# The tanh gate multiplied into the values and their bias once, and the sum of gated attention and x made by GpSimd instead of VectorE

## The reference

```python
x = x + tanh(g_xattn[0]) * attention(layernorm(x), ctx, ctx)   # 16 heads of 32, 128 keys
x = x + tanh(g_ffn[0])   * moe(layernorm(x))                   # shared expert + top 2 of 8 experts
```

## Time and profile before

| | |
|---|---|
| median of 3 executions | 1089.70 us (1083.06 to 1090.62) |
| the profiled execution | 1085.73 us, span 1083.5 us |
| TensorE busy | 1012.0 us, 93% |
| VectorE busy | 775.1 us, 72% |
| ScalarE busy | 500.1 us, 46% |
| GpSimd busy | 425.3 us, 39% |
| first pass | to about 590 us |

### The profile page before, as it was taken

One profiled execution on the slowest core, in us unless ns is written; L12 is line 12 of the kernel. 1 busy time (PEld: TensorE's weight loads), 2 busy tenths in 40 slices (PEclk: granted clock), 3 DMA queues, 4 the chain that ended last, 5 costly groups with the idle time before them and its releaser, 6 DMA issues.

```text
span 1083.5 us, 31212 instructions
## 1 busy us (share of the span) xinstructions
PE 1012.0 (93%) x10160; PEld 778.7 (72%) x10161; DVE 775.1 (72%) x2795; ACT 500.1 (46%) x1010; POOL 425.3 (39%) x606
## 2 busy tenths in 40 slices
PE   5889899999999999999996599999999999989997
PEld 4678889888899888899984355555555555578885
DVE  4577888887898888888776566666666666545656
ACT  2456555456566566666542344444444444311111
POOL 4333355454555565554533222222212221045553
PEclk9787899999999999999998799999999999999999
DMA  9502565742455433236225243333333334169987
GB/s 369 222 21 90 211 135 100 111 103 73 54 103 109 109 100 89 60 81 184 89 82 135 68 128 117 116 115 113 113 114 116 116 116 145 60 182 329 303 292 262
DMA packets 76754, 147.30 MB, mean 136 GB/s; under 512 B 20912, under 2 KB 23088, under 8 KB 73872
## 3 DMA queue, kind: packets, MB, share of 16 engines
q1 hardware_dynamic: 46800, 68.11, 25.4%
q0 software_dynamic: 12896, 35.58, 11.3%
q10 hardware_dynamic: 16992, 42.74, 10.2%
HBM read 94.04 MB, written 52.35 MB: 135 GB/s over the span
## 4 chain that ended last, share of the span: by engine, by line
PE 75%; DVE 9%; issue 6%; ACT 4%; DMA 3%; POOL 2%; another core or an unknown queue 1%; SPq 0%; ACTq 0%; POOLq 0%; DVEq 0%
PE bank L1217 10%; PE bank L1225 9%; PE bank L1226 9%; PE bank L1227 9%; PE bank L1325 8%; PE bank L1301 5%; PE bank L1275 5%; PE bank L1277 4%; PE bank L1276 4%; PE bank L1285 2%; PE bank L1342 2%; PE bank L1340 2%; PE bank L1341 2%; DVE arena L887 2%; PE bank L1287 2%
## 5 line engine op out<-in xcount | busy, mean ns | idle before, releaser
L1275 PE MATMUL bank<-arena,weights 128*128 128x128 f16 x1024 | 185.3, 225 | 13.5 <-DVE arena L1018 8.7
L1277 PE MATMUL bank<-arena,weights 128*128 128x128 f16 x1024 | 185.1, 225 | 0.0
L1276 PE MATMUL bank<-arena,weights 128*128 128x128 f16 x1024 | 185.1, 225 | 0.0
L1217 PE MATMUL bank<-ident,arena 128*128 128x128 f32 (+1 forms) x1336 | 179.5, 270 | 2.5 <-DMA arena<-normed_rows,arena 1.9
L579 POOL DMA_INDIRECT arena<-normed_rows,arena x71 | 69.1, 973 | 250.1 <-PE bank L1217 225.0
L1217 PEld LDWEIGHTS bank<-ident,arena 128*128 128x128 f32 (+1 forms) x1336 | 143.8, 141 | 23.8 <-DMA arena<-normed_rows,arena 2.5
L527 POOL TENSOR_TENSOR arena<-arena 128x512 f32<-128x512 f32 x96 | 101.0, 1052 | 142.7 <-DVE arena L887 135.1
L1325 PE MATMUL bank<-arena 128*128 128x33 f32 x1024 | 137.3, 280 | 7.6 <-ACT arena L622 7.6
L1325 PEld LDWEIGHTS bank<-arena 128*128 128x128 f32 x1024 | 131.4, 200 | 14.7 <-ACT arena L622 12.2
L887 DVE CUSTOM_DVE_ANT_0 arena<-bank,arena 128x128 f32<-128x128 f32 x512 | 116.9, 284 | 31.2 <-PE bank L1301 31.2
L622 ACT ACTIVATE arena<-bank 128x512 f32<-128x512 f32 x128 | 75.9, 593 | 115.5 <-PE bank L1217 108.2
(11 more groups left out here) (196 smaller groups left out, 2268.9 us busy)
## 6 DMA issues: line engine op xcount, KB each, us to landing
expert_rows<-arena ACTq DMA_DIRECT2D x71, 256.0 KB, 2.2
arena<-in_x SPq DMA_DIRECT2D x64, 256.0 KB
x_rows<-arena SPq DMA_DIRECT2D x48, 256.0 KB, 5.4
arena<-x_rows SPq DMA_DIRECT2D x48, 256.0 KB, 3.8
weights<-in_w_gu ACTq DMA_DIRECT2D x8, 1024.0 KB, 7.0
normed_rows<-arena SPq DMA_DIRECT2D x32, 256.0 KB, 5.6
out<-weights ACTq DMA_DIRECT2D x32, 256.0 KB, 4.5
weights<-in_w_down ACTq DMA_DIRECT2D x4, 1024.0 KB, 13.5
```

Source lines behind the costliest of these rows:

```text
L1217: last = t.transpose(dst[:, c * P:(c + 1) * P], src[:, c * P:(c + 1) * P], (ident16 if src.dtype == F16 else ident)[:, :])
L1275: t.matmul(at, shared(c, part, 0, dc), x_hi_c, start=(c == 0), stop=False)
L1276: t.matmul(at, shared(c, part, 0, dc), x_lo_c, start=False, stop=False)
L1277: last = t.matmul(at, shared(c, part, 1, dc), x_hi_c, start=False, stop=(c == EC - 1))
```

## The change

The gate goes into the values when they are made, once: GpSimd multiplies the bias `bv_s` by the gate (a new semaphore `bv_gated` tells VectorE), and VectorE's step that adds the bias to the values multiplies them by the gate too. The attention then comes out gated, and `x1 = attn + x_res` is a plain sum. GpSimd makes it, as the first step of its iteration, ahead of `shift(0)`. VectorE's L937 goes. Since VectorE now overwrites `attn` for the next tile while another engine reads it, `normalise` waits for `x1_ready`.

```diff
+            pool.wait_ge(gate_set, 2)
+            g.tensor_scalar(bv_s, bv_s, gate[:, 0:1], None, ALU.mult).then_inc(bv_gated, 1)
...
+                n, j, u = tile(J, v, LX1)
+                if live(n, NT):
+                    hold(pool, pool_passed, (res_here[u], 16 * (j + 1)))
+                    need(pool, x1_out[u], 16 * j)
+                    need(pool, xn2_ready, n - 1)
+                    pool.wait_ge(attn_done[0], n + 1)
+                    pool.wait_ge(attn_done[1], n + 1)
+                    g.tensor_tensor(x1[u], attn, x_res[u], ALU.add).then_inc(x1_ready, 1)
                 shift(0)
...
                 dve.wait_ge(kv_mm, 2)
+                dve.wait_ge(bv_gated, 1)
                 for b in range(B):
-                    last = d.tensor_tensor(vaug[:, b, :, 0:D], bank[6 + b][:, :].rearrange("p (h d) -> p h d", h=H),
-                                           bv_s.rearrange("p (h d) -> p h d", h=H), ALU.add)
+                    last = d.scalar_tensor_tensor(vaug[:, b, :, 0:D], bank[6 + b][:, :].rearrange("p (h d) -> p h d", h=H), gate[:, 0:1],
+                                                  bv_s.rearrange("p (h d) -> p h d", h=H), ALU.mult, ALU.add)
...
                         dve.wait_ge(inv_done[half], n + 1)
+                        need(dve, x1_ready, n)
...
-                if live(n5, NT):
-                    dve.wait_ge(res_here[u5], 16 * (j5 + 1))
-                    dve.wait_ge(attn_done[0], n5 + 1)
-                    dve.wait_ge(attn_done[1], n5 + 1)
-                    need(dve, x1_out[u5], 16 * j5)
-                    d.scalar_tensor_tensor(x1[u5], attn, gate[:, 0:1], x_res[u5], ALU.mult, ALU.add).then_inc(x1_ready, 1)
                 maxima(1)
...
                 if live(n5, NT):
-                    dve.wait_ge(x1_ready, n5 + 1)
+                    hold(dve, dve_passed, (x1_ready, n5 + 1))
                     d.bn_stats(stats2[u5], x1[u5]).then_inc(ln2_stats, 1)
```

## The result

Four executions of the changed kernel took 1101.87, 1106.01, 1106.13 and 1109.34 us, median 1106.07; the kernel before, four times on the same chip, 1086.64 (1083.06 to 1090.62). The ratio is 1.018, with its interval [1.012, 1.023]: the kernel is slower by 1.8%. The forecast was 1100 us. The profiled execution took 1106.01 us, 20.3 us more than that of before. In the ratios of the experiments, single executions over 1.5% above the fastest of their kernel are left out (two of kernel 8, one each of kernels 5 and 11); the medians and ranges hold all. Where the lines of the program have moved, the new number is given with the old one the first time.

The account below looks back on a forecast made before the run. The prediction took TensorE to bound the kernel, held up at times through GpSimd and ScalarE. Its terms, -0.7 + 8.2 + 6.8 = +14.3 us on the profiled 1085.7 us, gave 1100 us, range 1086 to 1110.

Parts of the forecast that it names:

- What bounds the loop: First-pass loop: TensorE sets the pace, sometimes held through GpSimd and ScalarE, with no slack in even iterations; wait 0.39 us.
- Taken off VectorE: Removing L937 from VectorE 32 times: nothing gained in the loop, -0.7 us in iteration 7, bounds 0 and -2.0.
- VectorE's busy time: In the first pass, VectorE's busy time was to fall by about 40 us with L937 gone.
- The sum on GpSimd: Ahead of GpSimd's first subtraction: sum of 1.05 us delays eight even loop iterations, +8.2 us, bounds 6.0 to 16.8.
- Outside the loop: Written-out iterations before and behind the loop: the added sum was counted as costing nothing there.
- The clock: Behind eight longer TensorE waits in the loop, four falls of the granted clock at 1.7 us, +6.8 us, bounds 0 to 13.6.
- The new wait of L901: VectorE's L901 must now wait for GpSimd's sum; claimed hidden by 0.2 us and the length of L899.
- The start: At the start, GpSimd's extra multiplication, VectorE's wait for it and L872's second operation, within 1.29 us for two, cost nothing.
- the clock holds: Rival: in the loop, waits of 1.44 us leave the granted clock at 1.00, giving 1093 us; chance 0.28.
- The second rival: In the loop, the clock falls nearly every time, or GpSimd's sum takes more than L527, giving 1107 us; chance 0.16.
- VectorE's relief reaches GpSimd: Rival: in even iterations GpSimd starts its sum 1.8 us earlier and TensorE's waits vanish, giving 1081 us; chance 0.07.

Follow-up runs that it names:

- kernel 8: The changed kernel with ScalarE's weight split moved to the odd iteration and GpSimd's mask steps behind its third subtraction; 1088.26 us, 1.001 of the kernel before.
- kernel 5: The changed kernel with the second operand of GpSimd's sum as 4 repeated columns instead of a full tile; 1095.92 us, 1.007 of the kernel before.
- kernel 11: The changed kernel with GpSimd's sum behind the second subtraction and ScalarE's weight split moved to the odd iteration; 1082.62 us, 0.996 of the kernel before.
- kernel 3: The kernel before plus a GpSimd sum of two idle tiles at the place of the change, VectorE keeping L937; 1101.38 us, ratio 1.015.
- kernel 6: The changed kernel with GpSimd's sum behind the second subtraction and two attn tiles in turn; 1084.88 us, 0.999 of the kernel before.
- kernel 7: The changed kernel with ScalarE's weight split moved from between the even iteration's exponentials to the odd iteration; 1101.63 us, 1.014 of the kernel before.
- kernel 2: The kernel before with gate and bias multiplied in as in the change, the sum staying on VectorE at its old place; 1086.22 us, ratio 1.003.
- kernel 9: The kernel before, sum on VectorE, with only ScalarE's weight split moved to the odd iteration; 1085.49 us, ratio 0.998.
- kernel 10: The kernel before, sum on VectorE, with ScalarE's weight split moved to the odd iteration and GpSimd's mask steps behind its third subtraction; 1079.44 us, ratio 0.995.
- kernel 1: The changed kernel run once more, unaltered; 1100.2 us, 1.017 of the kernel before.
- kernel 4: The changed kernel with GpSimd making the sum twice, once into a spare tile, at the same place; 1128.53 us, 1.036 of the kernel before.

## Why the prediction came out as it did

The forecast was 1100 us with a range of 1086 to 1110; measured were 1106. The mechanism was the predicted one, and two terms were too small: the length of the sum, and what is lost outside the loop, which was put at nothing. The 20.3 us found lie above the forecast's own bounds of +10 to +18 and within the range only by what was added for the spread of executions. In percent the forecast was +0.9 against a median of 1089.70 us of three executions; its +14.3 us are 1.3%, and 1.8% were measured.

- **What bounds the loop.** Right. The path GpSimd, ScalarE, TensorE without slack from the first subtraction on is shown by kernel 3, which costs 1.5% by delaying that point and nothing else, by kernel 6, which leaves that point alone and costs nothing, and by kernel 8, which keeps the sum ahead of that point, clears what lies behind it and costs nothing either. What the prediction did not see is a second path of nearly the same length through the second subtraction (kernel 7). It made no difference to the sum, since both start behind the added instruction.
- **Taken off VectorE.** Counted at nothing in the loop: right (kernels 6 and 11). L910, the old L899, waits 21.6 us for TensorE from 290 to 525 us, where L899 waited 13.0. In iteration 7 the forecast was 0.7 us of gain. L910 starts there at 103.12 instead of 104.11, and TensorE's L1424 (the old L1418 of the earlier trace rows) at 112.38 instead of 113.61, with 1.04 us of wait instead of 2.00. The gain of 1.2 us was lost at once: at `mix_values(2)` of iteration 9 the changed kernel is 2.3 us behind (145.83 against 143.57), and by iteration 15 the two traces stand nearly level (246.16 and 245.91). In between the clock is low for 20.5 us at a stretch, where it was low for 6.8 and 3.4 before:

```profile
113.00:133.40 20.40, 20.40 (x140) 18.99 (x139) 13.89 (x64) 9.68 (x19) 7.82 (x12) 0.50 0.59 236
```

- **VectorE's busy time.** Wrong: forecast about 40 us down, found 14.9. L937 and its 38.9 us are gone. But L938, the old L926, one addition of 128 x 8 elements, has become long. All its instances, shortest, median and longest ns, before and after:

```profile
L926 DVE TENSOR_TENSOR seen<-seen,arena x32: 148/153/221, 118.1 to 590.0; 128x8 f16<-128x8 f16 x32
```

```profile
L938 DVE TENSOR_TENSOR seen<-seen,arena x32: 147/154/2950, 116.6 to 609.5; 128x8 f16<-128x8 f16 x32
```

- In all it takes 20.3 us instead of 5.0: eight of the 32 take 1.7 to 2.95 us. Three other lines take 7.3 us more together (L963, the old L957, 3.4; L931, the old L919, 2.3; L898 1.7). The timeline of an odd iteration has VectorE's L938 beside GpSimd's two:

```profile
373.51 1.27 POOL L538 TENSOR_TENSOR arena<-arena 128x512 f32<-128x512 f32 x1
374.09 1.72 DVE L938 TENSOR_TENSOR seen<-seen,arena 128x8 f16<-128x8 f16 x1
374.74 1.04 POOL L529 TENSOR_TENSOR arena<-arena 128x512 f32<-128x512 f32 x1
```

- It starts 0.58 us into the sum and ends at 375.81, with the subtraction that follows (375.78). Before, L937 had lost 1.04 us of this kind, and the prediction noted it as done away with. It had looked only at L887 and L942 as new neighbours and passed over L926, which reads two tiles in SBUF. The loss moved to the next such instruction. The Trainium skill's page "SBUF — State Buffer", section "Who interferes with whom", says that such an instruction and a GpSimd one that reads SBUF hold each other off for a whole instruction; by that rule, the trace agrees, with the addition that VectorE got no turn between GpSimd's two. In kernels 2, 6, 9, 10 and 11, where GpSimd has no sum ahead of its first subtraction, the same line takes 4.9 to 5.1 us in all. The long L938 cost the loop nothing that can be seen: behind four of its five long instances there L910 still waited for TensorE, for 0.2 to 0.55 us, and behind the fifth (291.67) TensorE itself had no wait until 321.8.
- **The sum on GpSimd.** The step that was mis-sized. It was priced at 1.05 us by L527; it takes 1.28, since it reads two full tiles and L527 one and a repeated one (kernel 5: 1.077 us with a repeated operand). The prediction's 0.75 to 2.1 held it. Eight iterations were charged, and seven waited: iteration 18 did not, iteration 20 waited 0.56 us more than before, and the other six 1.23 to 1.58 more. 8.6 us measured stand against 8.2. That is closer than the parts are: a price too low by a fifth met a count too high.
- **Outside the loop** it was counted at nothing. That failed behind the loop: 4.7 us were lost between iteration 32 and the end of the pass. The fall at 536.3 and 2 x 3.4 us more of low clock at 584.1 and 601.1 would make 1.7 + 3.4 = 5.1 at the loop's price, so they are about all of it. The prediction's sum had no falls there. Ahead of iteration 18 it was nearly right: 1.5 us were lost.
- **The clock.** Four falls were forecast; there were three (399.7, 468.0, 536.3) in the one trace, four in the other. 1.7 us each was right: 27 matmuls made where 54 would be. Over the whole span the clock was low for 116.1 us where it was 88.6, and the odds of one in two were about what the loop shows (3 of 7 waits of 0.94 to 1.97 us). But the length of the wait before `mix_values(2)` isn't the whole condition: with waits of 1.33 us kernel 7 shows a fall behind five of six, and kernels 1, 7 and 8 one behind the wait of 0.96 to 0.99 us of L1307.
- **The new wait of L901** cost next to nothing, as forecast: L913 waited for the sum once in the whole trace, for 0.3 us. **The start** cost nothing that can be told (kernel 2), though L883 takes 1.41 us where 1.29 were forecast.
- **The rivals.** That the clock holds (1093) fell: it fell in each trace. The second rival (1107) is near the median. Its first form, that the clock falls nearly every time, isn't what happened: three and four falls, not eight. Its second form, that the sum takes more than L527, is true, by 0.25 us. That VectorE's relief reaches GpSimd (1081) is ruled out in the changed kernel by L910's waits, and in the kernels without the delay (6, 11) it brings nothing measurable.

**The ledger.** Forecast +14.3 us, found +20.3 between the two traces (+19.4 between the medians). The difference of 6.0 is: +0.4 for the waits (8.6 for 8.2); -3.4 for the falls in the loop, two between iterations 18 and 32 in place of four; +1.0 for the wait of L1307 and +0.4 for the rest there; +4.7 behind it; +2.2 ahead of iteration 18, where 1.5 were lost and 0.7 gained was forecast; +0.8 behind the first pass. That makes 6.1.

Open is why the stretch of low clock near 113 us is 17 to 20.5 us long in some kernels (the change twice, and kernels 5, 6, 10 and 11) and 7 to 10 in others (before, and kernels 2, 3, 4, 7, 8 and 9). It doesn't come with the sum on GpSimd alone, since kernel 10 has it without. No kernel was made to tell it, and since kernels 6, 10 and 11 are among the fastest here and kernels 3 and 7 among the slow ones, it does not decide the result. Open too is the wait of L1307 of about 1 us, which stands in the traces of the change and of kernels 1, 6, 7 and 8. Nor was it tried which of several equal waits the clock falls behind.

## What to carry to other kernels

An engine's share of the span says nothing about what one more instruction on it costs. GpSimd was 39% busy, and 1.28 us at the head of its iteration cost all of 1.3 us and falls of the clock beside, while the same instruction behind the second subtraction was free: look for the step that others wait for, and put new work behind it. Taking work off an engine that waits for the bounding one (L899's idle time, in the earlier trace rows) bought nothing that could be measured, and where TensorE waits behind two paths of like length, both have to be shortened before the loss comes back (kernels 7 and 8).

## What the runs showed of the hardware

- GpSimd's addition of 128 x 512 f32 values took 1.28 us with two full inputs, in the change as with two tiles that nobody else uses (kernel 3), and 1.08 us with one input repeated along the row (kernel 5); a subtraction with a repeated input took 1.04 us.
- A VectorE addition of 128 x 8 elements with both inputs in SBUF took 1.72 us instead of 0.15 beside two GpSimd instructions in a row, and up to 2.95 us elsewhere in the same trace.
- The granted clock fell to 0.5 behind three of the seven waits of 0.94 to 1.97 us in the change's loop, behind five of six waits of 1.33 us in kernel 7, and in all six pairs from 370 us on of kernel 4, with waits of 2.06 (the last 1.77) and 0.6 us. Behind the waits of 0.4 us of kernels 2 and 11 it did not fall; in kernel 10 it fell once, at 371 us, with one wait of 0.35 us 1.3 us before.
